# A Fourier layer on one core: the bias b1 added by TensorE, and the one-time work of image 0 handed to other engines

## The chip, the cores and the metric

One core of one Trainium2 chip. The metric is the device time of one execution in microseconds (us); the kernel before takes 442.46 us (median of 3 runs). Engines: TensorE (PE, weight loads PEld), VectorE (DVE), ScalarE (ACT), GpSimd (POOL), SyncE (SP, issues all loads and stores).

## The reference

x is 8 images of 32x32 pixels and 384 channels, fp32. With y the group norm of x (32 groups, groups of 12 channels):

```
bias = y @ bias_w.T + bias_b
X = rfft2(y), split into 4 blocks of 96 channels; real xr, imaginary xi
r1 = relu(xr @ w1[0] - xi @ w1[1] + b1[0])
i1 = relu(xr @ w1[1] + xi @ w1[0] + b1[1])
r2 = r1 @ w2[0] - i1 @ w2[1] + b2[0]
i2 = r2 @ w2[1] + i1 @ w2[0] + b2[1]
out = x + irfft2(r2 + 1j * i2) + bias
```

Since i2 uses r2, the kernel uses w2's product with its imaginary part, w2[0] @ w2[1] and w2[1] @ w2[1], and b2 reaches the output as a constant added to row 0 of the image (an impulse).

## The kernel before, in words

Large products are done in halves: a value is stored as a high and a low part in f16, and three matmuls (high x high, high x low, low x high) stand for one (mm3). ScalarE writes each high part out of a bank of PSUM, VectorE then the low part (value less high part).

Each engine runs its own program in the order written; semaphores tie them together. TensorE for image b:

- c1: nine units u, each 12 matmuls, of the width-transformed image y with w1, into three banks in turn. ScalarE (L907) and VectorE (L991) write z. p3_half(b, 0) is called ahead of unit 6.
- p1(b + 1, m), m = 0 to 5: the width transform of the next image, between them p3_half(b, 1) (at m = 0) and p3_last (at m = 2). ScalarE copies each p1 into yraw (y_copy, L867).
- p3: the height transform, 45 matmuls of 32x32 weights a half, units 0 to 3 and 4 to 7 in four banks each, unit 8 by itself. VectorE adds b1 (spectrum_sum, L1059) into rsum; ScalarE takes the relu as high part (r_high, L897), VectorE the low part (r_low, L1066).
- p4: eight groups j back over the height into rho (banks in turn), between them c2_bias, the product with bias_w; then c2_rho with w2, and p6, the transform back over the width. VectorE adds x (add_x). GpSimd has added bias_b and b2's row to x before (add_map, waits for the next image's statistics).

The last image has more=False: there is no p1 of a next image between its stages.

Once, ahead of image 0: the weights are scaled by powers of two. The maximum over the partitions is taken by GpSimd (all_peak) for w1 and b1 (s1), and again for w2 and bias_w (s2, second_scales, in image 0). VectorE makes b1's scaled copy (scale_b1), the two parts of w2's forms (second_forms, L1215 and L1218), b2row0 (shift_rows, L1225), and added (shift_all). TensorE multiplies b2row0 by w2imag ahead of image 0 (L812 to L817):

```
            pe.wait_ge(shift_in, 16 * N_SHIFT)
            pe.wait_ge(added_ready, 1)
            mm(c_bank[2][:, 0:CH], T("impulse", 2), b2rows[:, :], True, False, skip_group_check=True)
            ...
            image(0, 0, first=True)
```

In image 0 ScalarE also makes the high parts of bias_w (after y_copy 2, waits s2_ready) and of w2 (after y_copy 4).

## Time and profile before

| | us |
|---|---|
| median of 3 runs (442.2 to 443.78) | 442.46 |
| the profiled execution | 442.63 |
| its span | 440.8 |
| TensorE busy | 401.7 |
| VectorE busy | 315.6 |
| ScalarE busy | 225.6 |
| GpSimd busy | 84.4 |

The profile is one execution of the kernel; its span is the time between the first and the last instruction that it records, the rest lies around it. Busy time is an engine's own; a wait is idle time of an engine, with what ended it.

### The profile page before, as it was taken

To read this page: it belongs to the slowest core of one execution; us is meant where nothing else is said; L and a number is where in the kernel's file an instruction comes from. 1 tells how busy PE (TensorE), PEld (TensorE's weight loads), DVE (VectorE), ACT (ScalarE), POOL (GpSimd) and SP (SyncE) were. 2 spreads that over 40 slices of the span, in tenths; PEclk is the share of its full clock that TensorE was granted. 3 is DMA by queue.
4 is the path that set the end of the run, shared out by engine and by line. 5 is a ranking of instruction groups with operands and counts; after the bars stand their busy time and mean duration, and the time that the engine had idled before them with its cause. 6 is when DMAs were issued, how large, how long until landed. Compare 5 with 4: busy or idle time off the path is not lost.

```text
span 440.8 us, 19270 instructions
## 1 busy us (share of the span) xinstructions
PE 401.7 (91%) x8530; PEld 356.2 (81%) x8530; DVE 315.6 (72%) x768; ACT 225.6 (51%) x504; POOL 84.4 (19%) x72
## 2 busy tenths in 40 slices
PE   4429969998999999999999999999999899995996
PEld 4427859987898989988898989888898789883894
DVE  3684986777668686768668686868767676869424
ACT  2542577426653476426662566438652576436320
POOL 0000100630009000630027000710036000880000
PEclk9857969999999999999999999999999999999899
DMA  7770000053001700053001700161003500130004
GB/s 218 205 233 1 4 1 3 27 177 126 3 5 37 288 2 5 27 181 121 3 5 71 256 3 4 39 232 58 5 3 128 198 3 4 39 146 1 4 4 144
DMA packets 12567, 33.24 MB, mean 75 GB/s; under 512 B 4994, under 2 KB 6692, under 8 KB 12484
## 3 DMA queue, kind: packets, MB, share of 16 engines
q1 hardware_dynamic: 12484, 32.00, 20.8%
q8 instruction: 68, 1.11, 1.1%
q14 instruction: 15, 0.12, 0.1%
HBM read 16.26 MB, written 12.58 MB: 65 GB/s over the span
## 4 chain that ended last, share of the span: by engine, by line
PE 82%; DVE 9%; ACT 4%; issue 4%; DMA 1%; DVEq 0%; SPq 0%; ACTq 0%
PE bank L552 82%; DVE r L1066 2%; DVE rsum L1059 2%; DVE z L991 1%; DMA x_sb<-in_x 1%; DVE y L991 1%; ACT yraw L867 1%; ACT r L897 1%; ACT junk L875 1%; ACT z L907 1%; ACT biasw L901 1%; DVE g L1218 0%; DVE o_sb L1082 0%; ACT w2s L901 0%; ACT junk L878 0%
## 5 line engine op out<-in xcount | busy, mean ns | idle before, releaser
L552 PE MATMUL bank<-biasw,y 128*64 128x384 f16 x1152 | 112.8, 341 | 0.0
L552 PEld LDWEIGHTS bank<-biasw,y 128*64 128x64 f16 x1152 | 94.2, 196 | 3.1 <-DVE rsum L1059 0.3
L552 PE MATMUL bank<-w2s,rho 128*64 128x96 f16 x3072 | 85.0, 207 | 0.2 <-issue 0.2
L552 PEld LDWEIGHTS bank<-w2s,rho 128*64 128x64 f16 x3072 | 80.1, 109 | 4.4 <-issue 2.9
L853 POOL TENSOR_TENSOR x_sb<-x_sb,added 128x384 f32<-128x384 f32 x56 | 74.6, 1368 | 0.0
L907 ACT ACTIVATE z<-bank 128x384 f16<-128x384 f32 x72 | 35.2, 489 | 67.1 <-PE bank L552 66.5
L552 PE MATMUL bank<-tab,x_sb 128*128 128x128 f32 x384 | 53.5, 295 | 10.0 <-DMA x_sb<-in_x 6.2
L552 PE MATMUL bank<-w1R,y 128*128 128x192 f16 (+3 forms) x768 | 59.8, 228 | 3.1 <-issue 2.6
L552 PEld LDWEIGHTS bank<-tab,x_sb 128*128 128x128 f32 x384 | 49.2, 204 | 13.5 <-issue 7.0
L991 DVE SCALAR_TENSOR_TENSOR z<-bank,z 128x384 f16<-128x384 f32 x72 | 40.0, 557 | 28.1 <-ACT z L907 27.8
L851 POOL TENSOR_TENSOR x_sb<-x_sb,added 128x384 f32<-128x384 f32 x8 | 8.1, 1006 | 259.7 <-DVE yraw L1047 231.1
L892 ACT ACTIVATE g<-bank 128x384 f16<-128x384 f32 x64 | 30.2, 482 | 52.9 <-PE bank L552 52.9
L991 DVE SCALAR_TENSOR_TENSOR rho<-bank,rho 128x256 f16<-128x256 f32 (+2 forms) x128 | 40.0, 362 | 23.9 <-ACT rho L925 15.9
L552 PE MATMUL bank<-w1I,y 128*128 128x192 f16 (+1 forms) x384 | 53.3, 249 | 0.0
L1073 DVE SCALAR_TENSOR_TENSOR g<-g,bank 128x384 f16<-128x384 f16 x64 | 34.5, 548 | 20.9 <-ACT g L892 20.9
L552 PEld LDWEIGHTS bank<-w1R,y 128*128 128x128 f16 (+3 forms) x768 | 38.2, 98 | 7.7 <-issue 6.3
L991 DVE SCALAR_TENSOR_TENSOR y<-yraw,rstd,y 128x1024 f16<-128x1024 f32 x24 | 38.4, 1606 | 7.1 <-ACT y L887 7.1
L897 ACT ACTIVATE r<-rsum 128x384 f16<-128x384 f32 (+1 forms) x72 | 37.2, 519 | 10.0 <-DVE rsum L1059 9.2
L1066 DVE SCALAR_TENSOR_TENSOR r<-rsum,r 128x384 f16<-128x384 f32 (+1 forms) x72 | 37.3, 548 | 3.4 <-ACT r L897 2.8
L552 PEld LDWEIGHTS bank<-tab,r 64*128 64x128 f16 (+2 forms) x1536 | 28.5, 98 | 13.2 <-issue 4.7
L552 PE MATMUL bank<-tab,r 64*128 64x64 f16 (+2 forms) x1536 | 34.0, 197 | 5.5 <-DVE rho L991 4.0
L1059 DVE SCALAR_TENSOR_TENSOR rsum<-bank,b1s 128x384 f32<-128x384 f32 (+1 forms) x72 | 38.1, 546 | 0.0
(104 smaller groups left out, 433.0 us busy)
## 6 DMA issues: line engine op xcount, KB each, us to landing
x_sb<-in_x SPq DMA_DIRECT2D x16, 768.0 KB, 7.1
out<-o_sb SPq DMA_DIRECT2D x14, 768.0 KB, 3.8
y<-y SPq DMA_DIRECT2D x24, 128.0 KB, 2.7
out<-o_sb SPq DMA_DIRECT2D x8, 192.0 KB, 2.1
tab<-in_tab SPq DMA_DIRECT2D x1, 672.0 KB, 6.1
o_sb<-in_bias_wt SPq DMA_DIRECT2D x4, 144.0 KB, 2.9
b1s<-in_b1h SPq DMA_DIRECT2D x1, 384.0 KB, 5.2
tab<-in_tab SPq DMA_DIRECT2D x1, 291.5 KB, 3.0
```

Source lines behind the costliest of these rows:

```text
L552: return nc.tensor.matmul(o, lhsT, rhs, start=start, stop=stop, **kw)
L851: nc.gpsimd.tensor_tensor(tiles[:, 0, :], tiles[:, 0, :], added[:, 0, :], ALU.add).then_inc(x_shifted, 1)
L853: nc.gpsimd.tensor_tensor(tiles[:, t, :], tiles[:, t, :], added[:, 1, :], ALU.add).then_inc(x_shifted, 1)
L867: nc.scalar.activation(yraw[:, ct, :, :].rearrange("k a (m t) -> k (a m) t", t=TILES)[:, :, 4 * h:4 * h + 4], p1_bank[m % 2][:, :].rearran ...
L875: nc.scalar.activation(junk[:, 0:768].rearrange("k (a m) -> k a m", m=384), full_units(ct), ACT.Square, accum_out=sumsq[:, 0, ct:ct + 1]). ...
L892: nc.scalar.activation(g[:, 0, gi, :], g_bank(gi, more)[:, 0:CH], ACT.Copy, scale=G_EVAC).then_inc(gh_ready, 1)
L897: nc.scalar.activation(r[0:rows, 0, u, :], rsum[0:rows, u, :], ACT.Relu).then_inc(rh_ready, 1)
L907: nc.scalar.activation(z[:, 0, u, :], b_bank[u % 3][:, 0:CH], ACT.Copy, scale=Z_EVAC).then_inc(zh_ready, 1)
L991: return nc.vector.scalar_tensor_tensor(out=out, in0=value, scalar=factor, in1=high, op0=ALU.mult, op1=ALU.subtract)
L1059: nc.vector.scalar_tensor_tensor(out=rsum[0:rows, u, :], in0=spec_bank(u)[0:rows, 0:CH], scalar=H_EVAC, in1=b1s[0:rows, u // 4, :], op0=AL ...
L1066: nc.vector.scalar_tensor_tensor(out=r[0:rows, 1, u, :], in0=rsum[0:rows, u, :], scalar=0.0, in1=r[0:rows, 0, u, :], op0=ALU.max, op1=ALU. ...
L1073: nc.vector.scalar_tensor_tensor(out=g[:, 1, gi, :], in0=g[:, 0, gi, :], scalar=-1 / G_EVAC, in1=g_bank(gi, more)[:, 0:CH], op0=ALU.mult, ...
```

## The change

- b1 is no longer added by VectorE. b1's two rows are kept as f16 rows in every row group (b1rows: even rows the high part, odd rows what is left), and TensorE multiplies them by ones (b1ones) into the bank ahead of the height matmuls: four matmuls of 32x128 weights and 384 columns ahead of each p3_half, two of 32x64 ahead of p3_last. The tables are scaled by 8 instead of 32, and z's factor makes up for it, so that the bank holds the sum itself. rsum and spectrum_sum are gone; r_high and r_low read the bank, and the waits for spec_sum become waits for rl_ready.
- ScalarE and VectorE take the relus in another order: units 0 and 1 after z(5), 2 after z(6), 3 after z(7); ScalarE takes r(4), then r(5) and r(6), r(7), r(8) after the copies 0 to 3.
- b2's product moves from ahead of image 0 into c1, ahead of unit 3.
- ScalarE makes the first part of w2's forms, b2row0 and b1's signed and scaled copy (two passes); VectorE joins them in split_b1.
- GpSimd does only the two maxima until then; the small multiplications ahead of the second one are VectorE's. GpSimd also makes added's second map.
- largest_bias goes ahead of y_low, second_scales behind r_low(1), the high part of bias_w one copy earlier, that of w2 one copy earlier.
- The shift loads are issued ahead of image 1's; the two loads of b1 for unit 8 are gone.

```diff
-Z_EVAC = 2.0 ** -7
+P_SCALE = 8.0
+Z_EVAC = 2.0 ** -7 / P_SCALE
...
-            yield b1s[:, 0:2, :], b1h.rearrange("(o h) n -> o h n", o=1).to_broadcast([128, 2, CH])
-            for ri in range(2):
-                yield b1s[64 * ri:64 * ri + 64, 2, :], b1[ri].rearrange("(o b) n -> o (b n)", o=1).to_broadcast([64, CH])
+            yield b1raw[:, :, :], b1h.rearrange("(o h) n -> o h n", o=1).to_broadcast([128, 2, CH])
...
-            load(1, 1)
             with nc.allow_non_contiguous_dma(reason="one column of 96 per block"):
                 for dst, src in shift_loads():
                     sp.dma_start(dst, src).then_inc(shift_in, 16)
+            load(1, 1)
...
                 for u in range(9):
+                    if first and u == 3:
+                        shift_product()
...
+            def shift_product():
+
+                pe.wait_ge(shift_in, 16 * N_SHIFT)
+                pe.wait_ge(b2_ready, BLOCKS)
+                mm(c_bank[2][:, 0:CH], T("impulse", 2), b2rows[:, :], True, False, skip_group_check=True)
+                for blk in range(BLOCKS):
+                    last = mm(c_bank[2][:, BC * blk:BC * blk + BC], b2row0[:, blk, :], w2imag[:, blk, :], False, blk == BLOCKS - 1, skip_group_check=True)
+                last.then_inc(shift_prod, 1)
...
                     if first:
                         pe.wait_ge(tables_in, 16)
+                        pe.wait_ge(b1_ready, 6)
                         pe.wait_ge(w2_forms, 12)
-                        pe.wait_ge(added_ready, 6)
+                        pe.wait_ge(shift_ready, 2)
...
+                for slot in range(4):
+                    rows = slice(32 * slot, 32 * slot + 32)
+                    mm(spec_bank(4 * half + slot)[:, 0:CH], b1ones[rows, :], b1rows[rows, half, :], True, False, skip_group_check=True)
...
-                pe.wait_ge(spec_sum, 9 * b + 3)
+                pe.wait_ge(rl_ready, 9 * b + 3)
...
+                both = b1rows[0:32, :, :].rearrange("k h (b a n) -> k (h b) a n", b=2, a=2)
+                for ri in range(2):
+                    mm(spec_bank(8)[64 * ri:64 * ri + 64, 0:CH], b1ones[0:32, 0:64], both[:, :, ri, :], True, False, skip_group_check=True)
...
-            pool.wait_ge(second_largest, 2)
-            pool.wait_ge(s1_ready, 1)
-            do(nc.gpsimd.tensor_tensor(extreme[:, 2:4], extreme[:, 2:4], coef[:, 2:4], ALU.mult))
-            do(nc.gpsimd.tensor_scalar(extreme[:, 3:4], extreme[:, 3:4], s1[:, :], None, ALU.mult))
+            pool.wait_ge(peak_ready, 2)
             all_peak(extreme[:, 2:4], peaks2[:, :])
+            pool.wait_ge(shift_in, 16 * N_SHIFT)
+            for to, of in shift_columns(added[:, 1, :], bias_all[:, :]):
+                nc.gpsimd.tensor_copy(to, of).then_inc(added_ready, 1)
...
-                act.wait_ge(spec_sum, 9 * b + u + 1)
-                nc.scalar.activation(r[0:rows, 0, u, :], rsum[0:rows, u, :], ACT.Relu).then_inc(rh_ready, 1)
+                act.wait_ge(spec_prod, 9 * b + u + 1)
+                nc.scalar.activation(r[0:rows, 0, u, :], spec_bank(u)[0:rows, 0:CH], ACT.Relu).then_inc(rh_ready, 1)
...
-                    if u >= 6:
-                        r_high(b, u - 6)
+                    for v in {5: (0, 1), 6: (2,), 7: (3,)}.get(u, ()):
+                        r_high(b, v)
...
-                    r_high(b, m + 3)
-                    if first and m == 2:
+                    for u in {0: (4,), 1: (5, 6), 2: (7,), 3: (8,)}.get(m, ()):
+                        r_high(b, u)
+                    if first and m == 1:
                         act.wait_ge(s2_ready, 1)
                         weight_high(*bias_parts, bias_ready)
-                    if first and m == 4:
+                    if first and m == 3:
                         weight_high(*w2_parts, w2_ready)
...
+            for slot, tile, rows in W2_SLOTS:
+                nc.scalar.activation(w2_form(rows, 0, slot), by_group(w2raw[rows, :, tile, :]), ACT.Copy, scale=sign[rows, tile:tile + 1]).then_inc(w2_forms, 1)
             std(0)
...
+            act.wait_ge(shift_in, 16 * N_SHIFT)
+            for blk in range(BLOCKS):
+                nc.scalar.activation(b2row0[:, blk, :], T("row0", BC), ACT.Copy, scale=b2col[:, blk:blk + 1]).then_inc(b2_ready, 1)
+            act.wait_ge(b1_in, 16 * N_B1)
+            act.wait_ge(s1_ready, 1)
+            nc.scalar.activation(b1signed[:, :, :], b1raw[:, :, :], ACT.Copy, scale=s1half[:, :]).then_inc(b1_high, 1)
+            act.wait_ge(b1_high, 1)
+            nc.scalar.activation(b1signed[:, :, :], b1signed[:, :, :], ACT.Copy, scale=coef[:, 4:5]).then_inc(b1_high, 1)
...
                     if first and u == 3:
-                        largest_bias()
-                    if first and u == 4:
-                        scale_b1()
-                    if u >= 5:
-                        spectrum_sum(b, u - 5)
-
-                for u in range(4):
+                        split_b1()
+                        shift_row0()
+                    for v in {5: (0, 1), 6: (2,), 7: (3,)}.get(u, ()):
+                        r_low(b, v)
+                    if first and u == 5:
+                        second_scales()
+
+                for u in range(4, 9):
                     r_low(b, u)
...
+            def split_b1():
+
+                dve.wait_ge(b1_high, 2)
+                nc.vector.scalar_tensor_tensor(out=b1rows[:, :, :].rearrange("k a n -> k (a n)"), in0=b1raw[:, :, :].rearrange("k a n -> k (a n)"),
+                                               scalar=s1odd[:, :], in1=b1signed[:, :, :].rearrange("k a n -> k (a n)"), op0=ALU.mult, op1=ALU.add).then_inc(b1_ready, 1)
...
             scales(0)
+            largest_bias()
             for ct in range(NT):
                 y_low(0, 0, ct)
             second_forms()
-            shift_rows()
-            shift_all()
```

## Rows read from the trace of the kernel before

**Rows 1.** The page: busy time of each engine, and the chain by engine.

```profile
PE 401.7 (91%) x8530; PEld 356.2 (81%) x8530; DVE 315.6 (72%) x768; ACT 225.6 (51%) x504; POOL 84.4 (19%) x72
...
PE 82%; DVE 9%; ACT 4%; issue 4%; DMA 1%; DVEq 0%; SPq 0%; ACTq 0%
```

**Rows 2.** Waits: us in total, times, longest.

```profile
PE bank L552 <- DVE b2row L1225: 8.4, 1, 8.4
...
POOL peaks L835 <- PE bank L552: 5.8, 1, 5.8
```

**Rows 3.** Timeline of the prologue: start, us, engine, what, count [idle before].

```profile
24.17 3.23 ACT L887 ACTIVATE y<-yraw,rstd 128x1024 f16<-128x1024 f32 x3
25.43 3.68 DVE L991 SCALAR_TENSOR_TENSOR y<-yraw,rstd,y 128x1024 f16<-128x1024 f32 x3 [1.29 <-ACT y L887]
...
30.37 2.34 DVE L1218 SCALAR_TENSOR_TENSOR g<-bank,tab,o_sb 128x96 f32<-128x96 f32 x8
...
33.39 1.61 PE L552 MATMUL bank<-b2rows,tab 2*128 2x384 f32 x2 [8.35 <-DVE b2row L1225]
...
34.93 2.02 PE L552 MATMUL bank<-g,b2row 96*128 96x96 f32 x8
...
41.37 1.74 DVE L1252 TENSOR_REDUCE extreme<-g 128x1 f32<-128x1536 f32 x1
...
43.95 1.34 DVE L1257 TENSOR_REDUCE extreme<-o_sb 128x1 f32<-128x1152 f32 x1
```

**Rows 4.** Windows: stretch, length, each engine's busy time, PEclk, DMA.

```profile
36.50:39.50 3.00, 3.00 (x21) 2.84 (x20) 1.09 (x5) 0.49 (x1) 0.00 (x0) 0.50 0.00 0
39.50:44.00 4.50, 4.01 (x49) 3.81 (x47) 3.67 (x6) 1.96 (x4) 0.00 (x0) 0.99 0.00 0
...
56.00:58.00 2.00, 0.17 (x1) 0.17 (x2) 1.45 (x3) 2.00 (x3) 0.00 (x0) 0.65 0.00 0
```

**Rows 5.** Timeline of image 0, from the second maximum to p4.

```profile
52.47 0.37 POOL L835 PARTITION_ALL_REDUCE peaks<-extreme  x1 [5.80 <-PE bank L552]
...
54.96 2.34 ACT L901 ACTIVATE biasw<-o_sb,sbias 128x1152 f16<-128x1152 f32 x1 [0.64 <-DVE unscale L1265]
...
57.83 2.07 PE L552 MATMUL bank<-tab,x_sb 128*128 128x128 f32 x8 [2.71 <-ACT yraw L867]
...
62.02 1.81 DVE L991 SCALAR_TENSOR_TENSOR w2s<-g,s,w2s 128x1536 f16<-128x1536 f32 x1
...
64.62 1.11 PE L552 MATMUL bank<-tab,r 64*128 64x64 f16 x48 [0.63 <-DVE rho L991]
```

**Rows 6.** Timeline of image 2, TensorE: p3_half(0), p1, p4.

```profile
149.82 0.79 PE L552 MATMUL bank<-z,tab 32*32 32x384 f16 x45
...
158.85 2.06 PE L552 MATMUL bank<-tab,x_sb 128*128 128x128 f32 x16 [0.33 <-ACT yraw L867]
160.84 0.87 PE L552 MATMUL bank<-tab,r 64*128 64x64 f16 x48
161.65 1.74 PE L552 MATMUL bank<-biasw,y 128*64 128x384 f16 x18
163.41 1.11 PE L552 MATMUL bank<-tab,r 64*128 64x64 f16 x48
```

**Rows 7.** Timeline of the last image, TensorE: p3_half(1), p4, c2_bias.

```profile
399.07 0.78 PE L552 MATMUL bank<-z,tab 32*32 32x384 f16 x45 [0.69 <-DVE z L991]
...
407.76 1.41 PE L552 MATMUL bank<-tab,r 64*128 64x64 f16 x48 [3.37 <-DVE rho L991]
...
409.10 2.90 PE L552 MATMUL bank<-biasw,y 128*64 128x384 f16 x18
```

**Rows 8.** Groups by line and shape: busy us, mean ns of one.

```profile
L1059 DVE SCALAR_TENSOR_TENSOR rsum<-bank,b1s 128x384 f32<-128x384 f32 x56 | 29.4, 546 | 0.0
L897 ACT ACTIVATE r<-rsum 128x384 f16<-128x384 f32 x56 | 28.9, 519 | 8.8 <-DVE rsum L1059 8.3
L867 ACT ACTIVATE yraw<-bank 128x512 f32<-128x512 f32 x48 | 28.3, 590 | 9.7 <-PE bank L552 9.7
```

More of the change, by code:

```diff
@@ L165 @@
 TABW = TAB16W = 0
-for _name, _wide in (("width", 256), ("own", 128), ("block3", 128), ("const", 64), ("sign", 3), ("coef", 4), ("impulse", 128), ("row0", 128)):
+for _name, _wide in (("width", 256), ("own", 128), ("block3", 128), ("const", 64), ("sign", 3), ("coef", 6), ("impulse", 128), ("row0", 128)):
     TAB[_name] = (TABW, TABW + _wide)
@@ L488, in by_group, with shift_columns, split @@
             return v.rearrange("k b (i q) -> k b i q", q=3)
+        def shift_columns(to, *of):
+            def split(v, first, permuted):
+                if permuted:
+                    v = v.rearrange("k (c i q) -> k c i q", c=3, q=4)
+                    return v[:, :, :, 0:3] if first else v[:, :, :, 3]
+                if first:
+                    return v[:, 0:3 * BC].rearrange("k (c i q) -> k c i q", c=3, q=3)
+                return v[:, 3 * BC:CH].rearrange("k (i c) -> k c i", c=3)
+            return [[split(to, first, True)] + [split(v, first, False) for v in of] for first in (True, False)]
         block = ctx.enter_context(nc.Block())
@@ L655, in p3_half @@
                             last = mm(spec_bank(4 * half + slot)[32 * t:32 * t + 32, 0:CH], height[rows, w, 0, rows],
-                                      z[rows, of, 4 * half + t, :], of == 0 and w == 0, of == 1, skip_group_check=True)
+                                      z[rows, of, 4 * half + t, :], False, of == 1, skip_group_check=True)
                             if of == 1 and t == 2:
@@ L811, in _ @@
             last.then_inc(w2_prod, 1)
-            pe.wait_ge(shift_in, 16 * N_SHIFT)
-            pe.wait_ge(added_ready, 1)
-            mm(c_bank[2][:, 0:CH], T("impulse", 2), b2rows[:, :], True, False, skip_group_check=True)
-            for blk in range(BLOCKS):
-                last = mm(c_bank[2][:, BC * blk:BC * blk + BC], b2row0[:, blk, :], w2imag[:, blk, :], False, blk == BLOCKS - 1, skip_group_check=True)
-            last.then_inc(shift_prod, 1)
             image(0, 0, first=True)
@@ L1095, in image @@
                     if first and u == 3:
[L1096 to L1111 removed]
+                        split_b1()
[5 more added lines that the diff above has]
+                for u in range(4, 9):
+                    r_low(b, u)
+                    if first and u == 6:
                         bias_low(*bias_parts, bias_ready)
[L1113 to L1114 removed]
                 if first:
@@ L1160, in _ @@
             nc.vector.memset(newton[:, :], 0.0).then_inc(stored[1], 16)
+            nc.vector.memset(b1ones[:, :], 0.0).then_inc(b1_ready, 1)
+            dve.wait_ge(b1_ready, 1)
+            for slot in range(4):
+                nc.vector.memset(b1ones[32 * slot:32 * slot + 2, :], 1.0).then_inc(b1_ready, 1)
             steps = [0]
@@ L1209, in second_forms @@
                 dve.wait_ge(w2_prod, 1)
-                for part in range(2):
-                    for slot, tile, first_row, last_row in ((0, 0, 0, 128), (1, 1, 0, 64), (2, 1, 64, 128), (3, 2, 0, 128)):
-                        rows = slice(first_row, last_row)
-                        to, signs = w2_form(first_row, last_row, part, slot), sign[rows, tile:tile + 1]
-                        if part == 0:
-                            nc.vector.tensor_scalar(to, by_group(w2raw[rows, :, tile, :]), signs, None, ALU.mult).then_inc(w2_forms, 1)
-                            continue
-                        for half in range(2):
-                            nc.vector.scalar_tensor_tensor(out=to[:, half], in0=by_group(w2_product(tile)[rows])[:, half], scalar=signs,
-                                                           in1=by_group(w2real[rows, :, tile, :])[:, half], op0=ALU.mult, op1=ALU.add).then_inc(w2_forms, 1)
@@ new lines, in second_forms, with shift_row0 @@
+                for slot, tile, rows in W2_SLOTS:
+                    for half in range(2):
+                        nc.vector.scalar_tensor_tensor(out=w2_form(rows, 1, slot)[:, half], in0=by_group(w2_product(tile)[rows])[:, half], scalar=sign[rows, tile:tile + 1],
+                                                       in1=by_group(w2real[rows, :, tile, :])[:, half], op0=ALU.mult, op1=ALU.add).then_inc(w2_forms, 1)
+            def shift_row0():
+                dve.wait_ge(shift_prod, 1)
+                for to, of, product in shift_columns(added[:, 0, :], bias_all[:, :], c_bank[2][:, 0:CH]):
+                    nc.vector.tensor_tensor(to, of, product, ALU.add).then_inc(shift_ready, 1)
```

109 lines of the change are left out of this document (38 added, 71 removed).

## The prediction, made before the changed kernel was run

> **What bounds the kernel now.** I read the page first: TensorE is busy 91% of the span and holds 82% of the chain that ended last, VectorE 9%, ScalarE 4% [rows 1]. So VectorE's work is worth something only where TensorE waits for it, and I looked for those places by the view of waits and then by the timeline. There are three.
>
> (1) Prologue. TensorE waits 8.4 us for b2row0 [rows 2]: its product with the weights stands ahead of image 0, and VectorE comes to b2row0 only after the centred input and the forms of w2. The product then takes from 33.39 to about 36.7. The first stage (c1) could have begun when y_low(1) was done; the three y_low run from 25.43 for 3.68 us, 1.23 each, so at about 27.9 [rows 3].
>
> (2) End of image 0's first half. The second partition maximum on GpSimd comes 5.8 us late [rows 2], ends at 52.84, and the bias weights' high part cannot start before 54.96; it holds ScalarE for 2.34 us, and TensorE waits 2.71 us behind it for a copy of the next image [rows 5]. After that wait the granted clock fell: 0.99 in c1, 0.65 over 56 to 58, where it changes from 2.4 to 1.2 GHz [rows 4]; p4's third group starts at 64.62 [rows 5].
>
> (3) Last image. No p1 of a next image covers VectorE's 18 passes over the spectrum. TensorE waits 0.69 and, at p4's third group, 3.37 us, and the c2_bias behind it takes 2.90 us for what takes 1.74 in image 2 [rows 6, 7]: the lower clock again.
>
> Images 1 to 6 are TensorE's. In image 2 it waits 0.33 us in p1(4), and p4's third and fourth groups take 1.11 us where the first two take 0.87 [rows 6]: the fourth waits for VectorE's low part.
>
> **The change, middle images.** VectorE loses nine sums of 0.546 us an image [rows 8], 4.9 us, and each relu and its low part start one pass earlier. TensorE gains ten matmuls of 384 columns with 32 rows: four, in four row groups and banks, ahead of each p3_half, and two, in different columns, ahead of p3_last. None is in this trace. Nearest row: p3_half's 45 matmuls of 32x32, also 384 columns, stand at 149.82 for 0.79 with the last one's tail; the next stage starts about 0.72 after 149.82. Alone, each would stream 384 columns in 0.16 us at 2.4 GHz, together 7.2; so nearly all 16 tiles run together, in three rounds of 0.16, and 0.24 is passage [rows 6]. Four row groups of full width are then one round, 0.16; the two of p3_last one more. Three rounds are 0.48 an image. Bounds: nothing is no bound, since TensorE gets work; 0.48 is the floor. If the ten ran one by one at the 1.74/18 = 0.10 that a matmul in a pair costs in c2_bias, doubled because alone, it is 1.9; if each also waited out the one before it, ten records of 0.33 (the tail of a run, 0.79 less 0.46 of starts) are 3.3. I take 0.65, near the floor because the packed row is the same table on the same row groups; 0.17 is for a start of its own.
>
> The Trainium skill (TensorEngine Tiling (Array Packing), Key Properties) says that changing the tiling mode drains TensorE; by that rule each of the three groups pays another passage, as 32x128 is another mode than 32x32. Priced by the 0.24 of passage [rows 6], that makes 0.48 + 0.72 = 1.2 an image instead of 0.65. It is rival B below, which is also what the passage in the row would do by itself.
>
> Against the 0.65 stand the two waits, 0.33 + 0.09 of slower start and 0.24, together 0.66. They go if the engines behind them are earlier. I followed ScalarE's new order: after z(5) it makes r(0), r(1), then z(6), r(2), z(7), r(3), z(8), and in p1 the copies stand behind r(4); r(5), r(6); r(7); r(8). With 0.52 for a relu and 0.59 for a copy [rows 8] its third copy ends at about 158.9, and TensorE, 0.5 late, is done with p1(3) at 159.1: no wait. r(8) is now ahead of copies 4 and 5, so the first low part of rho is some 0.35 earlier and the fourth group finds it. Banks are held longer, until the low part (rl_ready) instead of the sum: units 0 and 1 are free about 1.5 us ahead of p3_half(1). Net 0 to +0.2 an image; for six, **+0.6** (from 6 x (0.48 - 0.66) = -1.1 to 6 x (1.2 - 0.66) = +3.2, and with 1.9, +7.4).
>
> **Prologue and image 0.** Moved on SP: the three shift loads go ahead of the 1.5 MB of image 1, and two b1 loads disappear; image 1's load is issued about as before and is not needed until about 43. Moved to ScalarE: four form parts, ahead of std(0), in time in which it is idle from 19.7 to 22.3 (1.4 us of work; cover 2.6; without it, if w2 were late, std(0) and all behind it slip up to 1.2). Then b2row0 (four of 0.3) and two passes over b1 (0.84 each) fill 27.4 to 30.3, ahead of z(0), which is ready at 30.4: free, but with no slack. On VectorE largest_bias (1.34 [rows 3] and two small steps) goes ahead of y_low, which had 1.3 idle waiting for y_high: +0.35. The five memsets of b1ones lie in the wait for tables: nothing.
>
> So c1 starts at 28.3 and not at 36.6. It does not keep all of that. Clock: at 0.99 c1 makes 49 matmuls in 4.0 us of work, 0.082 each; at 0.50 the window has 21 in 3.0, 0.143 [rows 4], which I round up to twice 0.082. A unit of 12 takes 1.0 or up to 1.9; units 0 to 2 end at about 33.7. The shift product, 3.2 us at half clock [rows 3], is 1.7 at full: 35.4. Units 3 to 5 end at 38.4. VectorE: y_low ends 29.5, eight product forms of 2.34 in all [rows 3] at 31.85, z low parts, largest_weight 1.74 and its two steps, z(3) at 37.6, then the new split_b1 (768 wide; 1.0, estimated from y_low's 1.23 for 1024) and shift_row0 (0.7) until 39.3. p3_half(0) waits for both: TensorE idle 0.9. Behind it in VectorE's queue stand z(4) and z(5), which units 6 and 7 need; they are just in time. p3_half(0) ends 40.3, unit 8 at 43.0, p1(0) at 44.0. VectorE makes r(0), r(1), then second_scales, whose maximum is long there: GpSimd does nothing else between its two maxima, and even if it were 5.8 late it would come at 41.5, before it is asked for. From the maximum's end to the bias part was 2.1 in rows 5; I take 1.7 for the nine steps, and z(7) ends at 45.5: wait 1.5. p3_half(1) 46.4, p1(1), p1(2), p3_last 49.3, p1(3) 50.3. ScalarE: after r(6), at 49.25, the bias part 2.34, copy 2 at 52.2: TensorE idle 1.9. p1(4), p1(5) 54.3; copy 4 stands behind r(8) and the w2 part and ends at 56.0: group 1 waits for it 1.3; c2_bias 58.2. VectorE's w2 part (1.81 [rows 5]) ends about 57.3 and the rho parts 58.6: the third and fourth groups are at 58.25 and 58.7, where they were at 64.62 and 65.2. **-6.5** (bounds: the whole 8.3 of an earlier c1; with one more stall of the size 2.71 and its clock, -3.5).
>
> **Last image.** p3_half(1) at 399.3 (0.25 later), then r(4) to r(8) only, one low part of 0.55 each instead of two passes: last one at 403.7 instead of 407.0. p4's first groups run from 402.85 to 403.6, rho's low parts from 403.9, the fourth group at 405.35 instead of 408.35: -3.0. TensorE's longest wait is then 1.1 instead of 3.37, so I expect no fall of the clock: 2.90 - 1.74 and 1.41 - 1.11 more [rows 6, 7], 1.5. **-4.5** (from -2.5 to -4.8).
>
> Sum: -6.5 + 0.6 - 4.5 = -10.4. The profiled execution took 442.63 with a span of 440.8; the three runs' median is 442.46, so they agree. 442.5 - 10.4 = **432**.
>
> **Rivals.** A, clock in image 0: waits of 1.5, 1.9 and 1.3 lie close together. Rows show falls after 2.71 and 3.37, none for 0.69 [rows 4, 5, 7]. If it fell at 52, p1(4), p1(5), the first groups and c2_bias, some 4.6 us of work less what waits anyway, cost about 2.3 more: 434.3. B, each group of bias matmuls pays a passage: + 0.55 x 8 = 4.4: 436.5. For it: the 0.24 is in the row; against: the tables, banks and row groups follow without change. C, image 0 gains half: ScalarE without slack, or w2 or shift data late, 3 us less: 435. D, the other side: the ten matmuls are not packed at all and each waits out the last, 3.3 an image; 8 x (3.3 - 0.65) = 21 more: 453. It decides from 0.65 + 10.4/8 = 1.95 an image upward; the packed 45 speak against. E, the two ends' gains come back: what was stalled becomes waits elsewhere (no other engine is near full: ScalarE 51% [rows 1]), or 1.9 an image: 442.
>
> **How the numbers follow.** Forecast 0.52, A 0.16, B 0.14, C 0.09, E 0.05, D 0.04. The predicted time is 432. The range 428.5 to 437.5 takes in the forecast with its end bounds (-3.5 at the ends with middle images at their floor), A, B and C, and leaves out D, E. A measurement of this kernel tells 0.5%, 2.2 us, from no change. Faster: forecast, A, B, C, 0.91; same 0.05; slower 0.04.
>
> **What the new profile would show.** c1's first matmul near 28 and no wait for b2row0; the second maximum near 36; image 0's fourth p4 group near 58.7; from c1 to c1 in the middle images the same within 0.2, with p1(4)'s wait gone; the four 32x128 matmuls starting within some 0.05 us of each other and p3_half with them 0.16 to 0.3 longer; a last image with no wait over 1.5 and the clock at 1.00. Wrong it would be by p3_half growing by 0.4 or more, by the clock at 0.5 between 45 and 60, or by copies of y coming later in every image because two relus now stand ahead of one.

## The result

The changed kernel takes 431.7 us (median of 4 runs, 430.86 to 432.9) against 442.61 (4 runs); the ratio is 0.9762, with a 95% interval of 0.9731 to 0.9793, so 2.4% faster. Forecast were 432.0 and a range of 428.5 to 437.5. The profiled execution took 432.9, with a span of 431.1, 9.7 less than before.

The page of the changed kernel, busy time and the chain by engine (beside [rows 1]):

```profile
PE 401.2 (93%) x8610; PEld 354.2 (82%) x8610; DVE 283.1 (66%) x696; ACT 228.9 (53%) x514; POOL 84.1 (19%) x72
...
PE 90%; ACT 4%; issue 2%; DVE 2%; DMA 1%; DVEq 0%; SPq 0%; ACTq 0%
```

TensorE has 80 more records (the ten b1 matmuls of eight images) and is busy as long as before; what shrank is its waiting. VectorE lost 72 instructions and 32.5 us, and its share of the chain fell from 9% to 2%. The waits of TensorE (us in total, times, longest; beside [rows 2]):

```profile
PE bank L571 <- ACT y L912: 3.2, 1, 3.2
...
PE bank L571 <- ACT yraw L892: 2.2, 2, 1.5
...
PE bank L571 <- ACT z L932: 1.7, 2, 1.0
PE bank L571 <- DVE rho L1029: 1.3, 1, 1.3
```

The 8.4 for b2row0 is gone; 3.2 for the centred input stands in its place, and the 3.4 for rho in the last image is 1.3.

Prologue and image 0 in the timeline of the changed kernel (beside [rows 3, 5]):

```profile
27.30 0.64 PE L571 MATMUL bank<-w1R,y 128*128 128x192 f16 x3 [3.23 <-ACT y L912]
...
32.03 0.91 PE L571 MATMUL bank<-b2rows,tab 2*128 2x384 f32 x2
...
34.34 0.35 POOL L859 PARTITION_ALL_REDUCE peaks<-extreme  x1 [21.14 <-DVE extreme L1262]
...
38.01 0.34 PE L571 MATMUL bank<-b1rows,b1ones 32*128 32x384 f16 x4 [1.04 <-ACT z L932]
...
43.85 0.34 PE L571 MATMUL bank<-b1rows,b1ones 32*128 32x384 f16 x4 [0.95 <-DVE z L1029]
...
47.27 2.37 ACT L926 ACTIVATE biasw<-o_sb,sbias 128x1152 f16<-128x1152 f32 x1
...
50.18 2.05 PE L571 MATMUL bank<-tab,x_sb 128*128 128x128 f32 x16 [1.52 <-ACT yraw L892]
...
53.35 0.52 PE L571 MATMUL bank<-tab,r 64*128 64x64 f16 x24 [0.66 <-ACT yraw L892]
...
55.66 1.11 PE L571 MATMUL bank<-tab,r 64*128 64x64 f16 x48
```

c1 begins at 27.30, with b2's product inside it at 32.03; four waits follow (1.04, 0.95, 1.52, 0.66), and p4's third group stands at 55.66, where it stood at 64.62 [rows 5]. The record at 38.01 is put down to ScalarE's z, which was done at 37.50; the last thing that p3_half(0) waits for is shift_row0 on VectorE, which ends at 37.70.

The clock in windows of the same kernel (beside [rows 4]; columns as there):

```profile
28.00:30.00 2.00, 2.00 (x15) 1.90 (x14) 1.97 (x7) 1.85 (x3) 0.00 (x0) 0.50 0.77 216
30.00:32.00 2.00, 2.00 (x21) 1.83 (x18) 1.28 (x5) 0.49 (x1) 0.00 (x0) 0.81 0.18 42
...
48.00:52.00 4.00, 2.48 (x22) 2.29 (x21) 2.47 (x4) 4.00 (x6) 0.00 (x0) 1.00 0.00 0
```

The clock rises to 2.4 GHz within 30 to 32, 3 to 4 us after c1 began, and stays there through the four waits.

A middle image (2), TensorE, from p1(0) and p3_half(1) to p4 (beside [rows 6]):

```profile
144.62 1.16 PE L571 MATMUL bank<-tab,x_sb 128*128 128x128 f32 x8
145.71 0.34 PE L571 MATMUL bank<-b1rows,b1ones 32*128 32x384 f16 x4
145.99 0.79 PE L571 MATMUL bank<-z,tab 32*32 32x384 f16 x45
146.70 2.05 PE L571 MATMUL bank<-tab,x_sb 128*128 128x128 f32 x16
148.68 0.35 PE L571 MATMUL bank<-b1rows,b1ones 32*64 32x384 f16 x2
148.97 0.66 PE L571 MATMUL bank<-z,tab 128*128 128x384 f16 x3
149.46 2.90 PE L571 MATMUL bank<-tab,x_sb 128*128 128x128 f32 x24
...
154.77 0.88 PE L571 MATMUL bank<-tab,r 64*128 64x64 f16 x48
...
157.25 1.76 PE L571 MATMUL bank<-tab,r 64*128 64x64 f16 x72
```

Four b1 matmuls together take 0.34 (the same four on all rows take 0.81 in e3), so they run side by side; from their start to the next stage's is 0.28, and 0.29 for the two of unit 8. p1(3) to p1(5) are one row of 24 without a wait, and p4's third and fourth groups take 0.88 instead of 1.11. Not all of that stays: the fifth and sixth groups, up to the c2_bias behind them, take 1.69 (157.25 to 158.94) where they took 1.45 (166.13 to 167.58).

The last image (beside [rows 7]):

```profile
392.81 0.34 PE L571 MATMUL bank<-b1rows,b1ones 32*128 32x384 f16 x4 [0.68 <-ACT z L932]
...
398.48 1.11 PE L571 MATMUL bank<-tab,r 64*128 64x64 f16 x48 [1.26 <-DVE rho L1029]
...
399.52 1.74 PE L571 MATMUL bank<-biasw,y 128*64 128x384 f16 x18
```

The wait of 3.37 is 1.26 and the c2_bias behind it takes 1.74 instead of 2.90: no fall of the clock. Over the ten executions of the changed kernel on record (these four and e12's six) the mean granted clock is 0.983 or 0.984, where the profiled execution of the kernel before has 0.965.

**Where the 9.7 us are.** I cut both traces at the same instructions: the second group mean (qv), c1's first matmul, image 0's third p4 group, the last image's first height matmul (p3_half(0)), its third and fifth p4 groups, and the span's end. The same cuts serve the experiments.

| stretch, us | before | changed | difference |
|---|---|---|---|
| start to qv (loads, first images of y) | 21.02 | 20.06 | -0.96 |
| qv to c1 | 15.73 | 7.24 | -8.49 |
| c1 to image 0's third p4 group | 27.87 | 28.36 | +0.49 |
| to the last image's p3_half(0) | 330.24 | 332.94 | +2.70 |
| to its third p4 group | 12.90 | 9.88 | -3.02 |
| to its fifth p4 group | 4.17 | 2.71 | -1.46 |
| to the end | 28.87 | 29.91 | +1.04 |

The first is chance: over all profiles here qv starts between 19.39 and 21.30, kernels alike. The last has a gap of 0.43 in TensorE's own issue, which one execution has here and another there; in e12, the same kernel again, it is 28.93. The middle holds such gaps too: 3.33 us before, 2.66 in the changed kernel, 1.58 in e12. A measure without them is the time from c1 to c1 of a clean image: 48.69 before, 48.99 changed (and in e12), so 0.30 more an image.

### The profile page after: what moved, and what is told of

Same layout as the page of the kernel before. It is cut to its first block, busy times and chain, and to the rows that moved or that the text cites. A ratio compares the mean times of both kernels' runs of the same rounds, so it can differ in the third digit from the quotient of the medians.

```text
span 431.1 us, 19365 instructions
## 1 busy us (share of the span) xinstructions
PE 401.2 (93%) x8610; PEld 354.2 (82%) x8610; DVE 283.1 (66%) x696; ACT 228.9 (53%) x514; POOL 84.1 (19%) x72
## 3 DMA queue, kind: packets, MB, share of 16 engines
q8 instruction: 68, 1.11, 1.1%
## 4 chain that ended last, share of the span: by engine, by line
PE 90%; ACT 4%; issue 2%; DVE 2%; DMA 1%; DVEq 0%; SPq 0%; ACTq 0%
PE bank L571 90%; DMA x_sb<-in_x 1%; ACT y L912 1%; ACT junk L900 1%; ACT yraw L892 1%; ACT r L922 1%; ACT biasw L926 1%; DVE o_sb L1114 0%; ACT w2s L926 0%; DVE r L1098 0%; ACT z L932 0%; ACT junk L903 0%; DVE rho L1029 0%; ACT rho L951 0%; DVE z L1029 0%
## 5 line engine op out<-in xcount | busy, mean ns | idle before, releaser
L571 PE MATMUL bank<-biasw,y 128*64 128x384 f16 x1152 | 111.1, 336 | 0.4 <-issue 0.4
L571 PE MATMUL bank<-tab,x_sb 128*128 128x128 f32 x384 | 50.6, 287 | 7.7 <-DMA x_sb<-in_x 6.2
L1098 DVE SCALAR_TENSOR_TENSOR r<-bank,r 128x384 f16<-128x384 f32 (+1 forms) x72 | 38.1, 552 | 27.6 <-ACT r L922 27.6
L571 PEld LDWEIGHTS bank<-tab,x_sb 128*128 128x128 f32 x384 | 47.4, 198 | 10.1 <-issue 7.4
L571 PE MATMUL bank<-w1I,y 128*128 128x192 f16 (+1 forms) x384 | 53.5, 249 | 0.0
L922 ACT ACTIVATE r<-bank 128x384 f16<-128x384 f32 (+1 forms) x72 | 33.1, 489 | 9.7 <-PE bank L571 9.7
L951 ACT ACTIVATE rho<-bank 128x512 f16<-128x512 f32 x48 | 27.5, 596 | 19.8 <-PE bank L571 19.6
L892 ACT ACTIVATE yraw<-bank 128x512 f32<-128x512 f32 x48 | 28.7, 601 | 16.9 <-PE bank L571 16.9
L1114 DVE SCALAR_TENSOR_TENSOR o_sb<-bank,unscale,x_sb 128x384 f32<-128x384 f32 x64 | 35.0, 610 | 3.4 <-PE bank L571 3.4
```

The costliest lines, as they stand in the source:

```text
L571: return nc.tensor.matmul(o, lhsT, rhs, start=start, stop=stop, **kw)
L892: nc.scalar.activation(yraw[:, ct, :, :].rearrange("k a (m t) -> k (a m) t", t=TILES)[:, :, 4 * h:4 * h + 4], p1_bank[m % 2][:, :].rearran ...
L922: nc.scalar.activation(r[0:rows, 0, u, :], spec_bank(u)[0:rows, 0:CH], ACT.Relu).then_inc(rh_ready, 1)
L951: nc.scalar.activation(rho_columns(0, j), rho_sums(bank), ACT.Copy, scale=H_EVAC).then_inc(rhoh_ready, 1)
L1098: nc.vector.scalar_tensor_tensor(out=r[0:rows, 1, u, :], in0=spec_bank(u)[0:rows, 0:CH], scalar=0.0, in1=r[0:rows, 0, u, :], op0=ALU.max, ...
L1114: nc.vector.scalar_tensor_tensor(out=o_sb[:, t, :].rearrange("k (p q) -> k p q", q=4), in0=o_bank[t % 4][:, 0:CH].rearrange("k (q p) -> k ...
```

## The experiments

All but e8, e9 and e12 are the changed kernel with one edit. Times are medians; "us" of the stretches come from each one's profile, cut as above.

| run | us | ratio to before, 95% | qv to c1 | c1 to p4 (0) | middle | last: to third group | to fifth |
|---|---|---|---|---|---|---|---|
| e1 no b1 matmuls | 426.08 | 0.9572 to 0.9677 | 7.25 | 28.14 | 326.89 | 9.52 | 2.72 |
| e2 b1 twice | 436.29 | 0.9807 to 0.9899 | 7.24 | 28.96 | 335.78 | 10.21 | 2.72 |
| e3 b1 on all rows | 437.09 | 0.9826 to 0.9912 | 7.24 | 29.61 | 335.26 | 10.35 | 2.72 |
| e4 VectorE loaded | 442.63 | 0.9962 to 1.0019 | 7.23 | 30.67 | 336.28 | 12.38 | 2.71 |
| e5 product ahead | 434.76 | 0.9798 to 0.9838 | 11.64 | 27.94 | 333.44 | 9.89 | 2.71 |
| e6 GpSimd multiplies | 431.55 | 0.9711 to 0.9782 | 7.24 | 28.51 | 330.75 | 9.88 | 2.71 |
| e7 longer wait | 433.53 | 0.9774 to 0.9816 | 7.24 | 30.68 | 331.97 | 9.88 | 2.71 |
| e8 before, VectorE multiplies | 442.93 | 1.0003 to 1.0044 | 15.71 | 27.79 | 330.26 | 12.91 | 4.48 |
| e9 old prologue parts | 439.52 | 0.9906 to 0.9971 | 16.06 | 27.64 | 331.84 | 9.88 | 2.71 |
| e10 old order of relus | 435.38 | 0.9776 to 0.9887 | 7.24 | 28.90 | 334.84 | 10.25 | 2.71 |
| e11 weights later | 429.37 | 0.9663 to 0.9768 | 7.24 | 27.65 | 332.59 | 9.88 | 2.71 |
| e12 changed again | 430.91 | 0.9689 to 0.9789 | 7.24 | 28.21 | 331.55 | 9.88 | 2.72 |

The middle stretch holds TensorE's issue gaps, which sum to between 0.3 and 3.3 us in a trace, so it tells half a microsecond only where rows of single images agree. It also holds image 0's third to fifth p4 group, 2.71 in most of these kernels but 4.10 in e8 and 4.13 in e10, where the clock fell. The profile is of one execution, and not always a typical one: e4's took 439.81 and e5's 437.39, with medians of 442.63 and 434.76.

e9 to e12 ran together, so their differences are taken against e12. It took 430.91, a little below the 431.7 within 0.7 that was expected of it.

### e1: the ten matmuls left out

The b1 term is left out of the result; the first height matmul opens each bank.

```diff
-                for slot in range(4):
-                    rows = slice(32 * slot, 32 * slot + 32)
-                    mm(spec_bank(4 * half + slot)[:, 0:CH], b1ones[rows, :], b1rows[rows, half, :], True, False, skip_group_check=True)
...
-                for ri in range(2):
-                    mm(spec_bank(8)[64 * ri:64 * ri + 64, 0:CH], b1ones[0:32, 0:64], both[:, :, ri, :], True, False, skip_group_check=True)
```

> The changed kernel without the ten b1 matmuls of each image (b1 is left out of the result); all else stays. Theory (each of the three groups costs 0.28 us from its first matmul to that of the group behind it, read in the changed kernel's trace, 0.83 an image, on TensorE's path in all eight images): about 6 us less than 431.7, some 425.5. Rival (the middle images' growth by 0.4 to 0.5 us has another cause, such as ScalarE's new order, and the matmuls are hidden): within 1 us of 431.7, and from c1 to c1 of clean middle images still 49.0.

426.08, 4.8 to 5.6 less than the changed kernel's two medians; the middle stretch is 5.4 shorter than the mean of the changed kernel's two profiles (332.94 and 331.55). They lie on TensorE's path in every image. A clean image takes 48.06 from c1 to c1, 0.93 less than in the changed kernel and 0.63 less than in the kernel before; so the matmuls cost 0.93 and the removed sums, with the new order of the relus, gave back 0.63. The starts of the three groups' rows show 0.28 + 0.28 + 0.29; the missing 0.10 stands ahead of unit 8's group, where p1(1) and p1(2) take 1.98 up to the next start instead of 1.88 or 1.89.

In image 0 of this profile the clock fell behind a wait of 1.89:

```profile
48.86 2.75 PE L571 MATMUL bank<-tab,x_sb 128*128 128x128 f32 x16 [1.89 <-ACT yraw L887]
```

```profile
50.00:52.00 2.00, 2.00 (x27) 1.77 (x27) 2.00 (x5) 2.00 (x4) 0.00 (x0) 0.51 0.00 0
```

### e2 and e3: what in the 0.28 is work, and what packing is worth

```diff
+                for again in range(2):
                     for slot in range(4):
                         rows = slice(32 * slot, 32 * slot + 32)
                         mm(spec_bank(4 * half + slot)[:, 0:CH], b1ones[rows, :], b1rows[rows, half, :], ...
```

> Every b1 matmul is issued twice in a row, the second overwriting the first. If 0.16 of the 0.28 us is the one packed round and the rest the passage to another tile shape, doubling adds 0.16 a group, 0.5 an image, 4 us: 435.6. If the whole 0.28 is work of the four matmuls, it adds 0.83 an image, 6.6: 438.3.

```diff
                 for slot in range(4):
-                    rows = slice(32 * slot, 32 * slot + 32)
-                    mm(spec_bank(4 * half + slot)[:, 0:CH], b1ones[rows, :], b1rows[rows, half, :], True, False, skip_group_check=True)
+                    mm(spec_bank(4 * half + slot)[:, 0:CH], b1ones[:, :], b1rows[:, half, :], True, False, skip_group_check=True)
```

> The four b1 matmuls ahead of each p3_half take all 128 rows (ones only in two of them, zeros elsewhere), so they are not packed, and stand in the same tile shape as c1; unit 8 as before. Theory (packing is worth three rounds of 0.16 a group): two groups of 0.64 and one passage less in place of two of 0.28, about +0.35 a group, +0.7 an image, +5.5: 437. Rival (packing brings nothing, the record's passage is the cost): the same 431.7 or less.

In e3 only the first row group of b1ones holds ones. TensorE's timeline in image 2, e2 first, then e3:

```profile
142.13 0.50 PE L571 MATMUL bank<-b1rows,b1ones 32*128 32x384 f16 x8
142.57 0.79 PE L571 MATMUL bank<-z,tab 32*32 32x384 f16 x45
```

```profile
147.74 1.16 PE L571 MATMUL bank<-tab,x_sb 128*128 128x128 f32 x8
148.73 0.81 PE L571 MATMUL bank<-b1rows,b1ones 128*128 128x384 f16 x4
149.47 0.79 PE L571 MATMUL bank<-z,tab 32*32 32x384 f16 x45
```

From the group's start to the next: 0.28 once, 0.44 twice, 0.74 or 0.75 on all rows. So a packed round of four is 0.16, and 0.12 of each group is not work of the matmuls. On all rows the four take 0.64 and 0.11 remain. Both times came out close to what was expected, 436.29 and 437.09.

The rows ahead of the groups say what the 0.12 goes with. On all rows the group has the shape of p1(0) before it and starts 0.99 after it (147.74 to 148.73); in the changed kernel it starts 1.09 after p1(0) (144.62 to 145.71), and so does the bare p3_half in the kernel before and in e1. Behind c1 it is the same, 0.25 instead of 0.34. All images without a wait or an issue gap there agree. So each change of tile shape on the way costs about 0.1: from 128x128 to 32x128 and on to 32x32 there are two, in e3 only one, as its expectation says. Unit 8's two matmuls of 32x64 stand between 128x128 stages and pay both. Bank and width of the weights are the same in e3, so they are not the cause. Packing a group of p3_half therefore saves 0.38 net (a clean image takes 49.75 in e3 against 48.99): 0.47 less work, 0.10 more passage.

### e4: VectorE's passes given back

```diff
+            def passed(b, u):
+                rows = BC if u in SHORT_UNITS else 128
+                dve.wait_ge(rh_ready, 9 * b + u + 1)
+                nc.vector.scalar_tensor_tensor(out=rsum[0:rows, u, :], in0=spec_bank(u)[0:rows, 0:CH], scalar=0.0, in1=r[0:rows, 0, u, :], op0=ALU.max, op1=ALU.add)
...
             def r_low(b, u):
+                passed(b, u)
```

> VectorE makes one more pass of about 0.55 us over every unit's bank ahead of its low part (as the removed sum, but nothing waits for its result and it is behind the relu); the b1 matmuls stay. Theory (the last image's gain is VectorE's removed passes): the last image's fourth p4 group about 3 us later and a fall of the clock there, +3 to +4.5; image 0 +1 to +2 more, because z's low parts stand behind the passes; the middle images +0.3 to +0.5 each: 438 to 441 in all. Rival (last image gained because relus no longer wait for a sum): under +2 in all, 433.

442.63: the whole gain is gone, more than expected. The profile is of a shorter execution, 439.81 at a mean granted clock of 0.984; seven of the ten took 442.3 to 443.2, at 0.973 to 0.981, so some 2.8 of the loss is not in it and goes with a lower clock at a place that no trace shows. The last image:

```profile
398.88 0.34 PE L572 MATMUL bank<-b1rows,b1ones 32*128 32x384 f16 x4 [1.75 <-DVE z L1030]
...
405.99 1.11 PE L572 MATMUL bank<-tab,r 64*128 64x64 f16 x48 [1.96 <-DVE rho L1030]
407.03 1.74 PE L572 MATMUL bank<-biasw,y 128*64 128x384 f16 x18
```

Of the last image's -3.02 up to the third group, 2.50 are lost again by the passes alone. In this execution the clock did not fall after 1.96, so the 1.46 behind it stayed. The rest went in image 0 (+2.3) and in the middle, where VectorE's passes now stand ahead of the z low part that p3_half(1) needs: a clean image takes 50.10, 1.11 more, and TensorE waits 12 times for z, 8.6 us in all. That is more than the 0.63 that taking the sums out gave, because the new order puts the passes of units 0 to 3 ahead of z's last low parts; e4 shows what VectorE's time costs in the changed kernel, and not what the sums cost in the old one.

### e5 and e9: the parts of the prologue undone

```diff
                 for u in range(9):
-                    if first and u == 3:
-                        shift_product()
...
             last.then_inc(w2_prod, 1)
+            shift_product()
             image(0, 0, first=True)
```

> The changed kernel with b2's product ahead of image 0 again (b2row0 stays on ScalarE, behind y_high). Theory: it waits for b2row0 until 27.6, then 3.2 us at the lower clock, so c1 begins near 30.8 instead of 27.3; units 3 to 5 follow without the product between them, and p3_half(0), which waited 1.04 at 38.0, starts near 38.5 to 39: +0.5 to +1.0 in all, 432.5. Rival (the move is what the prologue gained, 8 us of wait): +3 or more, 435 and up.

434.76, so 3.1 to 3.9 more: my estimate of 0.5 to 1.0 was wrong, the rival's right. The timeline of e5, from its longest execution (437.39):

```profile
29.03 1.61 PE L571 MATMUL bank<-b2rows,tab 2*128 2x384 f32 x2 [4.28 <-ACT b2row L995]
...
42.16 0.34 PE L571 MATMUL bank<-b1rows,b1ones 32*128 32x384 f16 x4 [1.11 <-ACT z L931]
42.43 1.01 PE L571 MATMUL bank<-z,tab 32*32 32x384 f16 x45
```

Counted from qv, the product starts 1.05 later than c1 does in the changed kernel, takes 3.35 at 1.2 GHz instead of 1.80 at 2.4, and c1 follows 4.40 later. Of these the stretch up to p4 wins back only 0.42, though the product is no longer in it. I had assumed that units 3 to 5 make it up; they could not: p3_half(0)'s wait in the changed kernel was only 1.04 long, and it is 1.11 again here, with another of 0.70 ahead of it, so VectorE had moved along.

```diff
-            for slot, tile, rows in W2_SLOTS:
-                nc.scalar.activation(w2_form(rows, 0, slot), ...
...
-                nc.scalar.activation(b2row0[:, blk, :], T("row0", BC), ACT.Copy, scale=b2col[:, blk:blk + 1]).then_inc(b2_ready, 1)
...
+                for slot, tile, rows in W2_SLOTS:
+                    nc.vector.tensor_scalar(w2_form(rows, 0, slot), by_group(w2raw[rows, :, tile, :]), sign[rows, tile:tile + 1], None, ALU.mult).then_inc(w2_forms, 1)
...
+            nc.vector.tensor_tensor(b2row0[:, :, :], row0, b2col[:, :].rearrange("k (b o) -> k b o", o=1).to_broadcast([BC, BLOCKS, 128]),
+                                    ALU.mult).then_inc(b2_ready, BLOCKS)
```

> As e5 (b2's product ahead of image 0), and besides w2's first form parts and b2row0 are VectorE's again, in their old place behind y_low; b1 stays on TensorE. Theory: c1 begins near 36.5 again as in the kernel before, 4 to 5 us later than in e5, of which image 0 keeps nearly all, since its later waits only move along: 438 to 439. Rival (image 0 is bound by the bias and w2 parts on ScalarE and VectorE): under +2 against e5, 436.

439.52, near the theory's 438 to 439. With these parts of the old prologue, everything else in the change (b1 on TensorE, the new order of the relus, the earlier bias and w2 parts) is worth 2.7 us against the kernel before (442.19 in this set); b2row0 and the form parts on ScalarE 4.8 more (e5, from another set); the product inside c1 another 3.9. b1 on TensorE by itself, with the old order and queues, was not run.

### e6 and e8: GpSimd's late maximum

```diff
-                nc.vector.tensor_tensor(extreme[:, 2:4], extreme[:, 2:4], coef[:, 2:4], ALU.mult).then_inc(peak_ready, 1)
+                nc.vector.memset(newton[:, 0:1], 0.0).then_inc(peak_ready, 1)
...
             pool.wait_ge(peak_ready, 2)
+            nc.gpsimd.tensor_tensor(extreme[:, 2:4], extreme[:, 2:4], coef[:, 2:4], ALU.mult).then_inc(pool_mult, 1)
+            pool.wait_ge(pool_mult, 1)
             all_peak(extreme[:, 2:4], peaks2[:, :])
```

> GpSimd does one small multiplication between its two maxima again. Theory (the second maximum then comes 5.8 us later, near 40.4 instead of 34.5, still ahead of second_scales, which asks at 40.6): no change, 431.7 within 0.5. Rival (the late maximum was image 0's cost): +2 or more.

e8 is the kernel before with its two multiplications moved to VectorE:

```diff
-            do(nc.gpsimd.tensor_tensor(extreme[:, 2:4], extreme[:, 2:4], coef[:, 2:4], ALU.mult))
-            do(nc.gpsimd.tensor_scalar(extreme[:, 3:4], extreme[:, 3:4], s1[:, :], None, ALU.mult))
...
+                do(nc.vector.tensor_tensor(extreme[:, 2:4], extreme[:, 2:4], coef[:, 2:4], ALU.mult))
+                nc.vector.tensor_scalar(extreme[:, 3:4], extreme[:, 3:4], s1[:, :], None, ALU.mult).then_inc(second_largest, 1)
```

> The kernel before, with one part of the change alone: the two small multiplications ahead of the second maximum are VectorE's. Theory: the second maximum is at about 46 instead of 52.5 and second_scales, in VectorE's queue, finds it at 53.2 as before, but not later; the bias part starts about as before: 0 to -0.5, near 442.3. Rival (image 0's wait of 2.71 and the fall of the clock came from the late maximum): -3 to -5, 438 to 439.

The second maximum in e6, and in e8 with what follows it:

```profile
33.59 0.19 POOL L867 TENSOR_TENSOR extreme<-extreme,tab 128x2 f32<-128x2 f32 x1 [20.34 <-DVE newton L1265]
39.91 0.37 POOL L860 PARTITION_ALL_REDUCE peaks<-extreme  x1 [6.13 <-issue]
```

```profile
43.97 0.35 POOL L835 PARTITION_ALL_REDUCE peaks<-extreme  x1 [30.85 <-DVE extreme L1257]
...
53.47 2.35 ACT L899 ACTIVATE biasw<-o_sb,sbias 128x1152 f16<-128x1152 f32 x1 [0.64 <-DVE unscale L1265]
56.35 1.16 PE L552 MATMUL bank<-tab,x_sb 128*128 128x128 f32 x8 [2.72 <-ACT yraw L865]
```

One multiplication costs the maximum 6.1 us, and neither run moves: 431.55, and 442.93 against 442.07. In e8 the maximum is there 9 us before the bias part, and TensorE waits 2.72 all the same. Keeping GpSimd clear of other work brings nothing here. (e8's profile has a second fall of the clock in image 0, behind a wait of 1.61, which costs 1.4 between the third and the fifth p4 group; its middle stretch hides that behind fewer issue gaps.)

### e7: the clock

```diff
                         weight_high(*bias_parts, bias_ready)
+                        nc.scalar.activation(spare[:, 0:768], tab[:, 0:768], ACT.Copy).then_inc(waited, 1)
+                        nc.scalar.activation(spare[:, 768:1280], tab[:, 0:512], ACT.Copy).then_inc(waited, 1)
```

> ScalarE copies 1280 more columns behind the high part of bias_w, about 1.5 us, so that TensorE waits about 3.0 instead of 1.52 us ahead of p1(4) in image 0. Theory (rows show the clock fall after waits of 2.71 and 3.37, not after 1.52): the clock falls to 1.2 GHz and +1.5 becomes +3 to +4: 435. Rival (the clock depends on something else): +1.5, 433.2, and granted clock 1.00 over 50 to 60.

```profile
52.55 3.48 PE L573 MATMUL bank<-tab,x_sb 128*128 128x128 f32 x16 [2.78 <-ACT yraw L894]
```

```profile
54.00:56.00 2.00, 2.00 (x12) 1.78 (x13) 1.17 (x2) 1.65 (x2) 0.00 (x0) 0.50 0.00 0
```

The wait is 2.78 and the clock falls, as the theory says; p1(4) and p1(5) take 3.48 instead of 2.05. But 433.53 is only 1.8 to 2.6 above the changed kernel, nearer to the rival's 433.2: the slower matmuls fill the 0.66 that p4 would have waited. In the profile the stretch is 2.3 to 2.5 longer. Of that 1.26 is wait and 0.5 to 0.7 is not from the edit (the clock rose later in c1, so p3_half(0) starts 11.22 after c1 instead of 10.71 or 10.54); only some 0.5 is left for the fall, and 0.2 of it comes back up to the fifth group (2.48 instead of 2.71).

### e10: the order of the relus

```diff
-                    for v in {5: (0, 1), 6: (2,), 7: (3,)}.get(u, ()):
+                    for v in {6: (0,), 7: (1,), 8: (2,)}.get(u, ()):
...
-                    for u in {0: (4,), 1: (5, 6), 2: (7,), 3: (8,)}.get(m, ()):
+                    for u in {0: (3,), 1: (4,), 2: (5,), 3: (6,), 4: (7,), 5: (8,)}.get(m, ()):
```

> The changed kernel with the relus (and their low parts) at their old places: unit 0 behind z(6), 1 behind z(7), 2 behind z(8), then one behind each copy of y. Theory (the relu reads the bank at once, so the order matters little once the sum is gone; unit 8's relu again stands behind the last copy, so rho's parts are 0.3 us later): +0.2 an image, 433. Rival (the new order does the work of keeping TensorE fed): p3_half(1) and p1(4) wait again, +0.5 an image and more, 436.

435.38, 4.5 above e12: the time is the rival's, but not the mechanism. In image 2 neither p3_half(1) nor p1(4) waits. p4's third and fourth groups are back at 1.11:

```profile
156.67 1.11 PE L571 MATMUL bank<-tab,r 64*128 64x64 f16 x48
```

The fifth and sixth are back at 1.46 as well, though, and a clean image takes 49.09 instead of 48.99: 0.1 an image, less than even the theory's 0.2. The loss is in image 0, where the clock fell behind a third wait in a row (0.69, 0.61, 1.64):

```profile
55.70 1.11 PE L571 MATMUL bank<-tab,r 64*128 64x64 f16 x48 [1.64 <-DVE rho L1029]
56.73 3.16 PE L571 MATMUL bank<-biasw,y 128*64 128x384 f16 x18
59.83 1.69 PE L571 MATMUL bank<-tab,r 64*128 64x64 f16 x72
```

c2_bias takes 3.16 instead of 1.74, and from the third to the fifth group it is 4.13 instead of 2.71. By the profiles image 0 loses 0.7 up to its third group and 1.4 behind it, the middle images 0.6, the last 0.4, and 1.1 is issue gaps (2.67 against 1.58). So the order matters for the two ends, not for the images between.

### e11 and e12: a later bias part

```diff
-                    if first and m == 1:
+                    if first and m == 2:
                         act.wait_ge(s2_ready, 1)
                         weight_high(*bias_parts, bias_ready)
-                    if first and m == 3:
-                        weight_high(*w2_parts, w2_ready)
...
                 for j in range(8):
+                    if first and j == 2:
+                        weight_high(*w2_parts, w2_ready)
...
+                    if first and j == 4:
+                        weight_low(*w2_parts, w2_ready)
```

> An attempt at a faster kernel: in image 0, the high part of bias_w one copy later (behind copy 2), so that p1(4) need not wait for it, and w2's parts in the idle time of p4 (high part ahead of group 2, low part ahead of group 4). Theory: p4's first two groups follow p1(5) without the 0.66 wait and p1(4) without its 1.52; c2_bias then waits for the bias low parts, which end at about 52.9 instead of 52.2: net -0.5 to -1.2, 430.8. Rival (c2_bias and the low parts of rho bound p4): 0.

> The changed kernel itself, on the same chip as e9 to e11, to compare them with: 431.7 within 0.7.

```profile
51.42 1.16 PE L571 MATMUL bank<-tab,x_sb 128*128 128x128 f32 x8 [1.47 <-ACT yraw L892]
```

The wait of 1.5 only moved from p1(4) to p1(5), still behind the bias part; the 0.66 ahead of p4's second group is gone, and the stretch is 0.56 to 0.71 shorter. 429.37 against 430.91 points the same way, but the intervals (0.9663 to 0.9768, 0.9689 to 0.9789) overlap: better by about 0.6 in the profile, not shown in the time.

## Why the prediction was right

**Qv to c1, -8.3 at most:** 8.49, that is c1 7.24 after qv. The wait for b2row0 was the prologue's bound, and the four form parts on ScalarE delayed nothing.

**Image 0, -6.5:** it came to -8.0 (8.49 less 0.49). The mechanism is there step by step, with waits of 1.04, 0.95, 1.52 and 0.66 where I had 0.9, 1.5, 1.9 and 1.3. Two terms were mis-sized. The clock rose at about 31, so units 0 to 2 and the product ended near 33.8 instead of 35.4 (34.4 with the 0.96 of the start taken off). And a relu out of the bank takes 0.49 instead of 0.52 out of rsum, two in a row 0.87, so the bias part began at 47.27 and not at 49.25 (48.3). I expected 1.8 of the early c1 to be given back; it was 0.5.

**What I had misread there:** part (2) put the late bias part in the kernel before down to GpSimd's late maximum. It is in the trace, but e8 shows that it cost nothing: with the maximum at 44.3, the bias part still starts only at 53.5, since second_scales stands in VectorE's queue behind the sums. The forecast did not use it, since it followed the queues.

**Middle images, +0.6:** they came to +2.7 by the profile (one b1 group of the last image in it), the step with the largest relative miss. The mis-sized term is the matmuls': 0.93 an image (e1) and not 0.65. What came back was 0.63, as forecast (0.66), though by another way: 0.87 up to p4's fourth group, of which the fifth and sixth lose 0.24 again. The net of 0.30 misses the sign that I had named, the same within 0.2 from c1 to c1. 6 x 0.30 + 0.28 is 2.1. The two profiles of the changed kernel stand 2.7 and 1.3 above the one before in this stretch; with their issue gaps taken off it is 0.46 to 0.52 an image, and why that is more than 0.30 stays open.

**The passage between tile shapes:** my 0.65 left this out. Three packed rounds are 0.48, and the rest of the 0.93 is four more changes of shape at about 0.11 each (one in each p3_half, two at unit 8). The Trainium skill's rule (TensorEngine Tiling (Array Packing), Key Properties) that changing the mode drains TensorE agrees with these rows: the passage appears and goes with the change of shape (e3). That the engine drains in it is not something a row here shows. So rival B's mechanism is what happened, at 0.45 an image instead of the 0.72 that I had put on it.

**Last image, -4.5:** -3.02 and -1.46, 4.48. e4 takes 2.5 of the first back with VectorE's passes; that the other 0.5 was the relu waiting for the sum is argued, not shown. The second is the clock.

**Rivals.** A did not happen in any of the ten executions of the changed kernel, but e7 makes it with a longer wait, and e1, e5 and e10 had it unasked: in e7 it costs some 0.3 to 0.5 because a later wait absorbs it, in e10 1.4. B's mechanism happened at 0.6 of its price, as above. D fell by the row of four matmuls in 0.34 and by e3: even on all rows the kernel is at 437. C and E did not happen. That the sum of 432.0 came so close to 431.7 is in part luck: image 0's extra 1.5 and the middle's lacking 2.1 nearly cancel.

## What to carry to other kernels

An elementwise pass costs what the slowest engine waits for it, stage by stage: nine passes an image were worth 0.63 us in images that another engine bounds, up to 3.0 in the last, uncovered one. Moving an addition into a matmul has a price on the bound engine, here 0.93 an image, half of it for changes of tile shape; in the middle images it lost 0.30 each, and with the ends it was worth 2.7 us together with the new order. Three quarters of the gain (8.6 of 11.3 against e12) came from one-time work that stood ahead of the first large stage. A late result counts only if its reader would have asked earlier: look in the reader's queue before blaming the writer. And before a stretch of a trace is compared, see whether the clock fell or the issue stopped inside it: both moved by more than the effects looked for.
